# Context attention: the score tile stored with queries outermost and the thirteen tiles side by side

## The reference

```
xn = layernorm(ctx_1024)                 # 32 x 1500 x 128
ln = layernorm(x)                        # 32 x 56 x 128, "latents"
q  = ln @ W_q                            # 2 heads of 64
kv = concat([xn @ W_kv, ln @ W_kv])      # 1500 + 56 keys
qn, kn = rmsnorm(q) * SCALE, rmsnorm(k)
sim  = einsum('bhid,bhjd->bhij', qn, kn)
sim  = where(mask, sim, -max)
attn = softmax(sim)
out  = einsum('bhij,bhjd->bhid', attn, v) @ W_out + b_out
```

## Time and profile before

| | |
|---|---|
| median of 3 runs | 1162.23 us (1154.1, 1162.23, 1166.36) |
| the profiled execution | 1154.43 us, span on the core 1152.7 us |
| PE busy | 968.5 us, 84% of the span |
| DVE busy | 967.9 us, 84% |
| ACT busy | 687.9 us, 60% |
| POOL busy | 605.6 us, 53% |
| granted PE clock, mean | 0.929 |

### The profile page before, as it was taken

The page is one execution under the profiler, slowest core; times in us unless marked ns, Lnnn a source line. Parts: engine busy times, 40 slices in busy tenths (PEclk is TensorE's granted clock), DMA queues, the critical chain, the costliest instruction groups (busy, mean ns, idle before and its releaser), DMA issues. The chain is left out here.

```text
span 1152.7 us, 21428 instructions
## 1 busy us (share of the span) xinstructions
PE 968.5 (84%) x7919; PEld 722.0 (63%) x7919; DVE 967.9 (84%) x1836; ACT 687.9 (60%) x1468; POOL 605.6 (53%) x827
## 2 busy tenths in 40 slices
PE   7889998387899999999999888691778777878796
PEld 5555654164799999999999756430333333645645
DVE  6989999958899999999997467678999999678475
ACT  5677765045566667667665355376656556267463
POOL 5600000014888888888885332102999999335270
PEclk8699999799899999999999999895889898989889
DMA  3000000021312112122100010002000000000001
GB/s 80 1 2 1 1 2 1 1 47 75 145 55 80 64 73 79 64 75 77 64 23 1 1 26 1 1 1 58 13 1 0 1 0 1 1 2 3 2 0 33
DMA packets 22717, 33.31 MB, mean 29 GB/s; under 512 B 9189, under 2 KB 17845, under 8 KB 22613
## 3 DMA queue, kind: packets, MB, share of 16 engines
q1 hardware_dynamic: 22101, 31.89, 8.5%
q10 hardware_dynamic: 512, 0.05, 0.0%
HBM read 31.02 MB, written 0.92 MB: 28 GB/s over the span
## 5 line engine op out<-in xcount | busy, mean ns | idle before, releaser
L2459 POOL TENSOR_TENSOR m_h_in<-m_dtu,xT 128x896 f32<-128x896 f32 x64 | 132.2, 2096 | 56.4 <-ACT xT L2480 56.4
L825 DVE SCALAR_TENSOR_TENSOR l0r_u<-l0r_u,l0r_a_col 128x1024 f32<-128x1024 f32 x110 | 136.1, 1278 | 4.9 <-ACT l0r_u L732 4.9
L2536 DVE TENSOR_TENSOR_SCAN m_hs<-msp_da,m_h_in 128x896 f32<-128x896 f32 x64 | 129.0, 2017 | 5.5 <-ACT msp_da L2498 4.9
L1299 POOL TENSOR_TENSOR bl_sc<-bl_sc,bl_topall 125x1456 f32<-125x1456 f32 x32 | 105.3, 3289 | 50.5 <-ACT bl_topall L1462 50.5
L732 ACT ACTIVATE l0r_u<-l0r_pu 128x512 f32<-128x512 f32 x218 | 108.8, 643 | 29.2 <-PE l0r_pu L632 29.2
L632 PE MATMUL l0r_pu<-l0r_xs,l0r_eb 32*128 32x256 f32 x896 | 104.5, 442 | 6.0 <-ACT l0r_u L732 3.9
L939 POOL MEMSET bq_lT<- 128x256 f32 x1 | 0.3, 312 | 190.6 <-POOLq L550 190.6
L1536 PEld LDWEIGHTS bl_pS<-b_qw,bl_xcT 128*125 128x125 f32 x768 | 99.1, 189 | 0.2
L1536 PE MATMUL bl_pS<-b_qw,bl_xcT 128*125 128x112 f32 x768 | 98.4, 271 | 0.0
L632 PEld LDWEIGHTS l0r_pu<-l0r_xs,l0r_eb 32*128 32x128 f32 x896 | 71.7, 201 | 38.5 <-ACT l0r_u L732 28.3
L2418 PE MATMUL msp_py<-m_hc,ident 128*128 128x448 f32 x192 | 92.7, 612 | 3.2 <-DVE mg_gT L2527 3.2
(11 more groups left out here) (426 smaller groups left out, 2368.2 us busy)
## 6 DMA issues: line engine op xcount, KB each, us to landing
b_xc<-in_ctx SPq DMA_DIRECT2D x16, 750.0 KB
bl_more<-in_ctx SPq DMA_DIRECT2D x16, 750.0 KB
x_tm<-in_x SPq DMA_DIRECT2D x1, 896.0 KB, 8.8
cw_cT<-in_ctx_headT SPq DMA_DIRECT2D x1, 896.0 KB, 4.6
out_dram<-x_tm SPq DMA_DIRECT2D x4, 224.0 KB, 2.5
l0r_xr<-in_x SPq DMA_DIRECT2D x4, 192.0 KB, 4.9
w_up<-in_L_ffn_w SPq DMA_DIRECT2D x1, 512.0 KB, 4.1
w_down<-in_L_ffn_w SPq DMA_DIRECT2D x1, 512.0 KB, 5.3
```

The lines of the kernel that those rows point to most:

```text
L825: ve.scalar_tensor_tensor(state(c, i, r), prev, a_col[:, :], state(c, i, r), ALU.mult, ALU.add).then_inc(s["step"], 1)
L1299: pool.tensor_tensor(sc[0:KP, n % 3, :, :], sc[0:KP, n % 3, :, :], over(topall[0:KP, n % 2, :].unsqueeze(1), [KP, KT + 1, QR]), ALU.subtra ...
L2459: pool.tensor_tensor(h_in[:, n % NI, :, :], dtu[:, k % 2, :, :], both_halves(bs[:, n % NB, :]), ALU.mult).then_inc(s["db"], 1)
L2536: ve.tensor_tensor_scan(hs[:, n % NS, :, :].rearrange("p h q -> p (h q)"), da[:, n % 2, 0:H2 * CH], h_in[:, n % NI, :, :].rearrange("p h q ...
```

## The change

The free dimensions of `sc` change places: [128, 3, QR, KT + 1] instead of [128, 3, KT + 1, QR]. The 13 numbers of one query now stand side by side (52 bytes), and the 112 queries follow each other at a step of 13 numbers. No instruction is added or dropped, and no wait or order changes. Every reader and writer gets other steps:

- `maximum` reads the tile straight, in runs of 13;
- `scale` writes with a step of 52 bytes from one element to the next (its loop stays k, h, q, for the sake of its PSUM input);
- `take_latents` writes and the second exponential reads with a step of 52 bytes;
- `subtract` goes straight over the tile, with each number of `topall` repeated 13 times in a row instead of the row of 112 repeated 13 times;
- the first exponential goes over 112 runs of 12;
- `mix` reads its moving operand with a step of 52 bytes;
- three memsets before the stage write with a step of 52 bytes.

```diff
-    sc = sb("sc", [P, 3, KT + 1, QR])
+    sc = sb("sc", [P, 3, QR, KT + 1])
...
-            fills = [(sc[:, buf, KT, :], NEG) for buf in range(3)] + [(top[96:P, buf, :], NEG) for buf in range(2)]
+            fills = [(sc[:, buf, :, KT], NEG) for buf in range(3)] + [(top[96:P, buf, :], NEG) for buf in range(2)]
...
                 pool.tensor_tensor(sc[0:KP, n % 3, :, :], sc[0:KP, n % 3, :, :],
-                                   over(topall[0:KP, n % 2, :].unsqueeze(1), [KP, KT + 1, QR]),
+                                   over(topall[0:KP, n % 2, :].unsqueeze(2), [KP, QR, KT + 1]),
                                    ALU.subtract).then_inc(s["subbed"], 1)
...
-                    ve.tensor_tensor(sc[0:KP, n % 3, tiles, :].rearrange("p k (h q) -> p k h q", h=HB),
+                    ve.tensor_tensor(sc[0:KP, n % 3, :, tiles].rearrange("p (h q) k -> p k h q", h=HB),
                                      pS[0:KP, u, 0:KS * QR].rearrange("p (k h q) -> p k h q", k=KS, h=HB),
                                      over(inv[:, n % 2, tiles, :].unsqueeze(3), [KP, KS, HB, L]),
                                      ALU.mult).then_inc(s["scaled"], 1)
...
-                ve.tensor_reduce(top[0:KP, n % 2, :], sc[0:KP, n % 3, :, :].rearrange("p k q -> p q k"), AX,
+                ve.tensor_reduce(top[0:KP, n % 2, :], sc[0:KP, n % 3, :, :], AX,
                                  ALU.max).then_inc(s["top"], 1)
...
-                act.activation(sc[0:L, n % 3, KT, :].rearrange("p (h q) -> p h q", h=HB), latS[:, n, :, :],
+                act.activation(sc[0:L, n % 3, :, KT].rearrange("p (h q) -> p h q", h=HB), latS[:, n, :, :],
                                ACT.Copy).then_inc(s["lats"], 1)
...
-                act.activation(sc[0:KP, n % 3, 0:KT, :], sc[0:KP, n % 3, 0:KT, :], ACT.Exp).then_inc(s["probs"], 1)
+                act.activation(sc[0:KP, n % 3, :, 0:KT], sc[0:KP, n % 3, :, 0:KT], ACT.Exp).then_inc(s["probs"], 1)
...
-                               sc[0:L, n % 3, KT, :].rearrange("p (h q) -> p h q", h=HB), ACT.Exp).then_inc(s["probs"], 1)
+                               sc[0:L, n % 3, :, KT].rearrange("p (h q) -> p h q", h=HB), ACT.Exp).then_inc(s["probs"], 1)
...
-                    last = pe.matmul(pO[:, mix_at], context(n)[:, t, :], sc[0:KP, n % 3, t, :],
+                    last = pe.matmul(pO[:, mix_at], context(n)[:, t, :], sc[0:KP, n % 3, :, t],
                                      start=(t == 0), stop=(t == KT - 1))
```

## The result

The changed kernel takes 1226.8 us (median of 4 runs, 1222.8 to 1231.3) against 1158.2 us for the one before (median of 4): 1.059 times as long, 95% interval 1.050 to 1.068. The forecast was 1224 us. The profiled execution has a span of 1226.2 us.

The account below looks back on a forecast made before the run. The prediction took PE to bound the context stage, with DVE's changes hidden. 768 `mix` records at +84 ns gave +64.7 us, on 1159.3 us a forecast of 1224 us; range 1175 to 1240, or 1150 to 1240 with rival A.

Parts of the forecast that it names:

- What bounds the stage: Context stage: PE sets the pace, busy 86.00 of 86.00 us, step 10.86 us; DVE is behind it by 8%.
- The spare room of `mix`: `mix` on PE: 112 ns a record, moving operand has 18 ns to spare and may take 1.0 ns a column.
- The term that decided, PE's stepped read: `mix` on PE: 1.75 ns a number as on DVE, 196 ns a record instead of 112, +64.7 us; chance 0.55.
- Maximum and subtraction: DVE's maximum 1.03 us shorter a step, at 1.67 us; POOL's subtract 2.75 us, or staying at 3.29.
- Scaling: DVE's stepped write: +0.39 us for each scaling of 448 numbers, +1.18 us for the three of a step.
- ACT: At most 0.1 us more for each small one, 2.4 us for the big one; ACT has idle time, so nothing.
- The total: Whole kernel: the average of four executions before, 1159.3 us, plus 64.7 us for `mix`, gives 1224 us.
- Signs that came otherwise: Profile after: DVE's idle time before the scalings up two us; a `mix` record's 275 ns up about as its pace.
- The rule of the Trainium skill that spoke for it: SBUF access: two or more hits per 16-byte line needed for full bandwidth; each access crossing to a new line pays.
- The rival from a page: Rival A, `mix` on PE: one column a cycle whatever the step, zero cost, 1154 to 1162 us; chance 0.34.

Follow-up runs that it names:

- the second experiment: Changed kernel, but `mix` reads 112 numbers side by side; DVE, POOL and ACT keep the change's steps: 1164.7 us, 1.003.
- the pairs: Changed kernel with the tile as 56 pairs of queries x 13 slabs x 2, so `mix` reads runs of two numbers: 1163.8 us, 1.003.
- The widths: Kernel before, `mix` from the second tile on reading 112, 96, 80, 64 or 32 columns at a 52-byte step: 28 to 30 ns less a record per 16 columns, 112 to 80.
- The bf16 run: Kernel before without the mask, its bf16 product reading 448 zeros at steps of 2, 4, 8, 12, 16 bytes: 0.19, 0.20, 0.39, 0.59, 0.78 us.
- the DVE experiment: Kernel before, `scale` and `maximum` at other steps by batch: 8 bytes free, full price at 16 (1.86 ns a number read), no more beyond.
- the old layout with the new mask: Kernel before, mask not by three bf16 products on PE but by POOL multiplying inverse deviation and shift with 0: 1150.4 us, 0.992.

## Why the prediction was right

- **What bounds the stage.** PE, without a gap. Shown by the second experiment and by the pairs: with pairs, DVE's maximum loses 1.03 us and POOL's subtraction 0.6 us a step with the scaling as before, and the step stays 10.87 us.
- **The spare room of `mix`.** 112 ns are set by the weight load and the moving numbers may take 1.0 ns each. The widths bear it out: at 1.75 ns each, 64 stepped numbers take the 112 ns of the weight load, and from 64 to 32 columns the record hardly gets shorter.
- **The term that decided, PE's stepped read.** Taken from two DVE reductions with steps of 128 and 448 bytes, 1.75 ns a number, 196 ns a record. Measured: 196 ns, step +2.05 us, stage +64.7 us. The trace of before had no stepped read on PE, so this was a choice between 0 and 1.93 ns; the argument was that DVE's price is no multiple of its own pace and so belongs to the memory. The bf16 run supports that argument: the price is that of a line, 1.75 ns, on both engines and on PE for both types. Nothing before the change promised a match to the nanosecond; the forecast's own range for this term went from 1.2 to 1.93 ns.
- **Maximum and subtraction.** 1.67 us and 2.75 us (at most 3.29) forecast, 1.67 and 2.68 measured.
- **Scaling.** Mis-sized: +0.39 us forecast from a write with a step of 224 bytes, +0.32 measured at 52. In the DVE experiment the writes cost 1002 ns at 16 bytes and 957 at 48, so the size of the step has a small part in it. It changed nothing, as DVE's idle time shows.
- **ACT.** 0.1 us for each small one, as the upper bound had it; the big exponential in runs of 12 is free.
- **The total.** 1159.3 + 64.7 = 1224 against 1226.8. The profiled executions differ by 73.5 us, 64.7 of them between the first and the last `take_mix`. Of the other 9, 7 lie ahead of these and 2 behind. The first `mix`, ahead of them too, accounts for 2; the rest is in stages that the change does not touch, and the runs of one kernel differ by as much.
- **Signs that came otherwise.** The forecast had DVE's idle time before the scalings up by two us. It went up by 0.5 us a step there (19.1 to 35.7 us over 32 batches) and by 1.4 before `overall` (L1384, 3.5 to 48.9), which waits for PE's `turn_peaks`: the sum was right, the place was not. The latency of a `mix` record went from 275 to 374 ns and more, 99 and not 84.
- **The rule of the Trainium skill that spoke for it** (SBUF — State Buffer, cachelines): two hits a line of 16 bytes suffice, each new line costs. The traces agree for f32: a step of 8 bytes is free for `mix` and for DVE, 16 bytes cost 1.79 ns on PE. For bf16 on PE two hits are not enough: 8 bytes, two numbers a line, double the product.
- **The rival from a page** (the Trainium skill, TensorE: Matmul & The Clock Gate, step by step, FILL: purely N cycles). The traces bear it out while the operand comes fast enough, at 0.42 to 0.44 ns a column for bf16 with a step of 2 or 4 bytes. With 8 bytes and more in bf16, or 12 and more in f32, the step of the operand sets the time.

## What to carry to other kernels

Before a layout is turned to please one reader, price the step of every reader and writer, and weigh each against the engine that sets the pace: here a reader with slack gained 1.03 us and the reader on the bound lost 2.05. In these runs a new line of 16 bytes cost 1.75 to 1.82 ns on PE's moving operand, 1.8 to 2.1 on its stationary one, and 1.75 to 1.9 on DVE. The f32 `mix` hides two numbers to a line behind its weight load; the bf16 product lost nothing with four to a line and half its speed with two. Interleaving in pairs gives both readers what they need; but a gain on an engine that is not the bound did not shorten the step, here not even after 0.5 us had been taken off the one that is.

## What the runs showed that I had not expected

- The price of a line holds for the weight load too: 234 ns a record at a step of 16 bytes, where straight it is 112. At 48 bytes it is 270, with the clock at 1.00.
- The clock can fall though PE shows no idle time. It did so in or right behind the first two `mix` with a stationary step of 48 bytes (0.57 from 638 to 642 us, 0.53 from 652 to 655), and the transposes behind each, read straight, took 1.87 us instead of 1.02. At a step of 16 bytes, 234 ns a record, it stayed at 1.00. That the slow weight load is the cause is likely but not shown.
- At the end of the stage the clock decides over 1.6 us. The last interval between two `take_mix` is 5.13 us with the clock at 1.00 in the kernel before, and 6.76 or 6.77 us with 0.72 in three others: the changed kernel with a straight `mix`, the pairs with the old mask, and the old layout with the new mask. No delay of the stage explains it: with the pairs and the old mask the three intervals ahead of it are 9.49, 8.46 and 5.14 us, in the kernel before 9.48, 8.45 and 5.13. The cause is open, and each of these is one execution.
- For PE's moving operand and for DVE, steps of 16 and 32 bytes cost slightly more than 48, 52 or 448: 1.79 and 1.82 ns a number against 1.78 and 1.75 on PE, 2851 ns against 2703 for DVE's maximum. For the stationary operand it is the other way round. The cause is open.
